# Two cross attentions on one core: another order of GpSimd in the first body, another cut of the last two

## The reference

```
stage 0: q = x Wq + bq; k = ctx Wk + bk; v = ctx Wv + bv
         w = softmax(q k^T / sqrt(512), over the query rows)
         n = layernorm(w v + x) * gamma + beta
stage 1: Q = n Wq + bq; K = ctx Wk + bk; V = ctx Wv + bv
         out = n + softmax(Q K^T / sqrt(512), over the keys) V Wo + bo
```

## Time and profile before

| | us |
|---|---|
| median of 3 runs | 681.7 |
| lowest, highest | 680.34, 682.13 |
| the profiled execution | 679.73 |
| its span | 677.8 |
| TensorE busy in the span | 666.5 |
| VectorE, GpSimd, ScalarE busy | 518.8, 490.5, 425.8 |

### The profile page before, as it was taken

How to read it: one execution, slowest core, us unless ns; L and a number is a source line. 1 busy time by engine, 2 the same in 40 slices (tenths; PEclk the granted TensorE clock), 3 DMA queues, 4 the chain that set the end, 5 groups by cost and what they waited for, 6 DMA issues and landing times.

```text
span 677.8 us, 12474 instructions
## 1 busy us (share of the span) xinstructions
PE 666.5 (98%) x4085; PEld 590.3 (87%) x4085; DVE 518.8 (77%) x1224; ACT 425.8 (63%) x1040; POOL 490.5 (72%) x394
## 2 busy tenths in 40 slices
PE   8998999999999999999999999999999999999997
PEld 7976988988898898889889898988989898888975
DVE  4978787877878687787968777796877779687764
ACT  4676657576665756666565666656566665666542
POOL 0387968779595877859687786958778695966771
PEclk9999999999999999999999999999999999999999
DMA  8902105050310405031040504004050401302003
GB/s 288 316 3 78 32 1 172 1 171 0 113 58 4 166 0 170 0 127 43 12 158 0 170 0 140 30 22 148 0 170 0 151 20 37 134 0 78 1 1 124
DMA packets 35585, 53.21 MB, mean 79 GB/s; under 512 B 5616, under 2 KB 13808, under 8 KB 35568
## 3 DMA queue, kind: packets, MB, share of 16 engines
q1 hardware_dynamic: 35568, 53.00, 23.7%
HBM read 36.18 MB, written 16.81 MB: 78 GB/s over the span
## 4 chain that ended last, share of the span: by engine, by line
PE 91%; POOL 4%; DVE 3%; issue 1%; DMA 1%; ACT 1%; SPq 0%; POOLq 0%; ACTq 0%; DVEq 0%
PE bank L424 79%; PE bank L431 12%; POOL n L1306 1%; POOL xprod L1333 1%; DMA wq_sb<-in_L_xattn_Wq_dram 1%; POOL wq_sb L1311 1%; POOL x_even L1347 0%; DVE rb L1059 0%; POOL cn_even_lo L1297 0%; POOL prod L1324 0%; DVE wv_sb L963 0%; DVE stats L1132 0%; POOL y_lo L1339 0%; POOL rstd L1317 0%; DVE x_even L1127 0%
## 5 line engine op out<-in xcount | busy, mean ns | idle before, releaser
L1324 POOL TENSOR_TENSOR prod<-n,u_b 128x512 f32<-128x512 f32 x64 | 81.5, 1295 | 40.1 <-DVE n L1143 39.2
L937 DVE SCALAR_TENSOR_TENSOR y_lo<-bank,terms,y_hi 128x512 fp32r<-128x512 f32 x64 | 47.9, 748 | 62.6 <-ACT y_hi L725 62.6
L1363 POOL TENSOR_TENSOR r<-r,beta_b 128x512 f32<-128x512 f32 x60 | 75.8, 1296 | 0.0
L1356 POOL TENSOR_TENSOR r<-n,gamma_b 128x512 f32<-128x512 f32 x60 | 75.5, 1286 | 0.1
L1317 POOL TENSOR_TENSOR rstd<-var_eps,minus_half 128x2 f32<-128x2 f32 x32 | 22.4, 699 | 65.4 <-DVE var_eps L1139 65.4
L725 ACT ACTIVATE y_hi<-bank,terms 128x512 fp32r<-128x512 f32 x64 | 43.9, 687 | 39.2 <-PE bank L424 39.2
L727 ACT ACTIVATE pc_hi<-bank 128x512 fp32r<-128x512 f32 x32 | 19.2, 600 | 68.4 <-PE bank L424 68.4
L813 ACT ACTIVATE bank<-e,neg 128x256 f32<-128x256 f32 x64 | 30.0, 469 | 37.9 <-DVE neg L1078 37.9
L424 PE MATMUL bank<-xT_hi,wqk_hi 128*128 128x512 f32 x128 | 51.2, 400 | 2.5 <-DVE xT_lo L939 2.5
L1116 DVE SCALAR_TENSOR_TENSOR r<-bank,rinv,r 128x512 f32<-128x512 f32 x60 | 44.8, 747 | 8.8 <-PE bank L424 8.8
L424 PE MATMUL bank<-wv_hi,wc_hi 128*128 128x512 f32 x128 | 51.5, 402 | 0.0
(11 more groups left out here) (214 smaller groups left out, 2381.4 us busy)
## 6 DMA issues: line engine op xcount, KB each, us to landing
out_dram<-r SPq DMA_DIRECT2D x15, 1024.0 KB, 5.5
x_even<-in_x_dram SPq DMA_DIRECT2D x8, 1024.0 KB, 7.3
ctxn<-in_ctx_dram SPq DMA_DIRECT2D x16, 512.0 KB, 3.7
x_odd<-in_x_dram SPq DMA_DIRECT2D x8, 1024.0 KB, 7.1
rb<-r_rows SPq DMA_DIRECT2D x15, 256.0 KB, 4.1
wq_sb<-in_L_xattn_Wq_dram SPq DMA_DIRECT2D x4, 256.0 KB, 5.2
wv_sb<-in_L_xattn_Wv_dram SPq DMA_DIRECT2D x2, 512.0 KB, 8.1
wq_sb<-in_L_xattn_Wq_dram SPq DMA_DIRECT2D x1, 1024.0 KB, 11.8
```

The lines of the kernel that those rows point to most:

```text
L937: i = dve.scalar_tensor_tensor(dst, src, bias, high.bitcast(F32), ALU.add, ALU.subtract)
L1324: pool.tensor_tensor(prod[j % 2][:], N[:, j, :], u_b[1][:], ALU.mult).then_inc(prod_ready, 1)
L1356: pool.tensor_tensor(r[:, j, :], N[:, j, :], gamma_b[:], ALU.mult).then_inc(scaled_ready, 1)
L1363: pool.tensor_tensor(r[:, j, :], r[:, j, :], beta_b[:], ALU.add).then_inc(resid_ready, 1)
```

## The change

On GpSimd the fourth column product of the first body goes to the other three; the larger sum of `bvwo` goes ahead of the first `rstd`, the smaller one behind it; the row products go ahead of the second `rstd`. VectorE's `finish_beta` of the first body goes to its end, and two preparation tiles take banks 6 and 7.

In the body before last `out` 0 is computed with its high products first, `n` of blocks 0 and 1 comes from ScalarE as rstd * x + shift, where VectorE makes shift = -mean * rstd. In the last body `late` 2 is computed in two halves, one ahead of and one behind the scores, the first quarter of the scores starts with its high products, `late` 3 takes bank 4, both low parts of `pt` go ahead of its output, and the last tile is computed, finished and stored in two halves of 256 columns in two banks.

```diff
--- before.py
+++ after.py
@@ -52,7 +52,7 @@
 PREP1B = tiles("wqk1", 2)
 PREP1C = [("wvo", 0), ("u1", 0), ("c1", 0), ("wvo", 1), ("bo1", 0)]
 
-PREP_BANKS = (7, 0, 1, 2, 3, 4, 5, 6) + (0, 1, 2, 3, 4, 5) + (2, 3, 6, 7) + (3, 1, 0, 5, 4)
+PREP_BANKS = (7, 0, 1, 2, 3, 4, 5, 6) + (0, 1, 2, 3, 4, 5) + (2, 3, 6, 7) + (3, 1, 0, 6, 7)
 
 
 def place_banks():
@@ -88,11 +88,12 @@
 FIRST = PREP0 + FIRST
 
 LATE = (1, 2, 3)
-BANK["late", 1], BANK["late", 2], BANK["late", 3] = 5, 0, 1
+BANK["late", 1], BANK["late", 2], BANK["late", 3] = 5, 0, 4
 BEFORE_LAST = [t for t in STEADY if t[0] != "out" or t[1] not in LATE]
 LAST = insert_after([t for t in STEADY if t[0] not in FRONT], ("nT", 3), [("late", 1)])
 LAST = insert_after(LAST, ("y1", 1), [("late", 2)])
-LAST = insert_after(LAST, ("pt", 0), [("late", 3)])
+LAST = insert_after(LAST, ("pt", 0), [("late", 3)]) + [("end", 0)]
+BANK["end", 0] = 0
 
 
 class Iteration:
@@ -241,7 +242,7 @@
         stats = sb("stats", [P, J, 6])
         mv = sb("mv", [P, J, 2])
         var_eps = sb("var_eps", [P, J])
-        rstd = sb("rstd", [P, J])
+        rstd, shift = sb("rstd", [P, J]), sb("shift", [P, RT])
         waited = sb("waited", [P, 2])
         minus_half = sb("minus_half", [P, J])
 
@@ -272,6 +273,7 @@
         bias_ready, x_biased = sem("bias_ready"), sem("x_biased")
         stats_ready, mv_ready = sem("stats_ready"), sem("mv_ready")
         var_ready, rstd_ready, n_ready = sem("var_ready"), sem("rstd_ready"), sem("n_ready")
+        shift_ready = sem("shift_ready")
         prod_ready, r1_ready = sem("prod_ready"), sem("r1_ready")
         negmx1_ready, neg1_ready, rinv1_ready = sem("negmx1_ready"), sem("neg1_ready"), sem("rinv1_ready")
         scaled_ready, resid_ready = sem("scaled_ready"), sem("resid_ready")
@@ -392,14 +394,19 @@
                     for j in range(J):
                         wait_emptied(sp, *((it, "late", j) if j in LATE else (before_last, "out", j)))
                     sp.dma_start(rows_of(out_rows, (PAIRS - 2) * J * P), R[:]).then_inc(rows_in_or_stored, 16)
-                    for j in range(J):
+                    for j in range(J - 1):
                         wait_emptied(sp, it, "out", j)
                         start = ((PAIRS - 1) * J + j) * P
                         sp.dma_start(out_rows[start:start + P, :], residual_of(it)[:, j, :]).then_inc(last_stored, 16)
+                    start = (PAIRS * J - 1) * P
+                    for tile, cols in ((("out", J - 1), slice(0, D // 2)), (("end", 0), slice(D // 2, D))):
+                        wait_emptied(sp, it, *tile)
+                        sp.dma_start(out_rows[start:start + P, cols], residual_of(it)[:, J - 1, cols])\
+                            .then_inc(last_stored, 16)
 
             run(sp, iteration)
             sp.wait_ge(rows_in_or_stored, 16 * (ROWS + PAIRS - 1))
-            sp.wait_ge(last_stored, 16 * J)
+            sp.wait_ge(last_stored, 16 * (J + 1))
 
 
         @block.tensor
@@ -602,12 +609,23 @@
             def scores1(it):
 
                 ct = CT[1 - it.parity]
-                for c in range(KC):
-                    wait_emptied(pe, it, "y1", c)
+                if it.last:
+                    pe.wait_ge(hi["y1"], it.times(KC, 0))
+                else:
+                    for c in range(KC):
+                        wait_emptied(pe, it, "y1", c)
                 for b in range(2):
                     dst = begin(it, "s1", b)
                     for tt in range(RT):
                         t0 = b * T + tt * P
+                        if it.last and (b, tt) == (0, 0):
+                            part = dst[:, 0:M]
+                            high, low = [h[:, :, t0:t0 + P] for h in Y1]
+                            product(part, [(high[:, c, :], h[:, c, 0:M]) for c in range(KC) for h in ct], last=False)
+                            for c in range(KC):
+                                wait_emptied(pe, it, "y1", c)
+                            product(part, [(low[:, c, :], ct[0][:, c, 0:M]) for c in range(KC)], first=False)
+                            continue
                         terms = []
                         for c in range(KC):
                             terms += passes([h[:, c, t0:t0 + P] for h in Y1],
@@ -654,6 +672,37 @@
                     terms += passes([h[:, b, ct, tt * P:(tt + 1) * P] for h in left], [h[:, ct, :] for h in right])
                 end(product(dst[:], terms), name, j)
 
+            def late_half(it, j, ct):
+
+                b, tt = divmod(j, RT)
+                dst = begin(it, "late", j) if ct == 0 else at(("late", j))
+                mm = product(dst[:], passes([h[:, b, ct, tt * P:(tt + 1) * P] for h in PC],
+                                            [h[:, ct, :] for h in WVO]), first=ct == 0, last=ct == KC - 1)
+                if ct == KC - 1:
+                    end(mm, "late", j)
+
+            def first_output(it):
+
+                pe.wait_ge(hi["pc"], it.times(2, 1 - 2))
+                dst = begin(it, "out", 0)
+                left = [[h[:, 0, ct, 0:P] for h in PC] for ct in range(KC)]
+                right = [[h[:, ct, :] for h in WVO] for ct in range(KC)]
+                product(dst[:], [(l[0], r[n]) for l, r in zip(left, right) for n in range(2)], last=False)
+                wait_emptied(pe, it, "pc", 0)
+                end(product(dst[:], [(l[1], r[0]) for l, r in zip(left, right)], first=False), "out", 0)
+
+            def last_output(it):
+
+                j = J - 1
+                b, tt = divmod(j, RT)
+                for tile, cols in ((("out", j), slice(0, D // 2)), (("end", 0), slice(D // 2, D))):
+                    dst = begin(it, *tile)
+                    terms = []
+                    for ct in range(KC):
+                        terms += passes([h[:, b, ct, tt * P:(tt + 1) * P] for h in PC],
+                                        [h[:, ct, cols] for h in WVO])
+                    end(product(dst[:, cols], terms), *tile)
+
             def iteration(it):
                 begin_it = it.j is None and it.known == 0
                 if begin_it:
@@ -679,13 +728,16 @@
                 if it.back:
                     project(it, "y1", "nT", WQK[1], NT)
                 if it.last:
-                    apply(it, "late", 2, "pc", PC, WVO)
+                    wait_emptied(pe, before_last, "pc", 1)
+                    late_half(it, 2, 0)
                 if it.front:
                     weigh0(it, 0)
                     row_sums(it)
                     weigh0(it, 1)
                 if it.back:
                     scores1(it)
+                if it.last:
+                    late_half(it, 2, 1)
                 if it.front:
                     if begin_it:
                         pe.wait_ge(wv0_ready, 1)
@@ -708,8 +760,13 @@
                 if begin_it:
                     prepare1c(it)
                 if it.back:
-                    for j in range(LATE[0] if it.before_last else J):
-                        apply(it, "out", j, "pc", PC, WVO)
+                    if it.before_last:
+                        first_output(it)
+                    else:
+                        for j in range(J - 1 if it.last else J):
+                            apply(it, "out", j, "pc", PC, WVO)
+                    if it.last:
+                        last_output(it)
 
             pe.wait_ge(consts_ready, 1)
             warm_up(0, 5)
@@ -837,6 +894,15 @@
                 wait_emptied(act, it, "rs")
                 act.activation(bias[j], bv0_b[:], ACT.Copy, scale=rs[:, j:j + 1]).then_inc(bias_ready, 1)
 
+            def normalise_first_rows(it):
+
+                wait_filled(act, it, "nT", KD - 1)
+                act.wait_ge(scaled_ready, it.times(J, 0))
+                act.wait_ge(shift_ready, 1)
+                for j in range(RT):
+                    act.activation(N[:, j, :], XN[it.parity][:, j, :], ACT.Identity, scale=rstd[:, j:j + 1],
+                                   bias=shift[:, j:j + 1]).then_inc(n_ready, 1)
+
             def row_terms(it, blocks, back):
 
                 for j in blocks:
@@ -916,6 +982,8 @@
                         round_bank(it, "pt", b, halves(PT[0], b))
                     for b in range(2):
                         round_bank(it, "pc", b, halves(PC[0], b))
+                        if it.before_last and b == 0:
+                            normalise_first_rows(it)
                 if it.more and it.back:
                     next_row_terms0(it)
                 if it.front and it.back and not it.before_last:
@@ -1116,6 +1184,15 @@
                 dve.scalar_tensor_tensor(r[:, j, :], at((name, j))[:], rinv1[:, j:j + 1], r[:, j, :],
                                          ALU.mult, ALU.add).then_inc(emptied[BANK[name, j]], 1)
 
+            def last_output(it):
+
+                r = residual_of(it)
+                for tile, cols in ((("out", J - 1), slice(0, D // 2)), (("end", 0), slice(D // 2, D))):
+                    wait_filled(dve, it, *tile)
```

(31 more changed lines are left out.)

## The result

| | before | changed |
|---|---|---|
| median of 20 runs | 681.49 us | 686.89 us |
| lowest, highest | 680.06, 682.13 | 680.17, 690.75 |
| profiled execution, span | 679.73, 677.8 | 689.38, 687.4 |

The ratio is 1.0051, 95% interval 1.0033 to 1.0069: slower. It leaves out the changed kernel's three runs over 690.5 us, which by their clock are more of what follows (the medians of all runs stand at 1.0079), as the ratios further down leave out two runs of before at 892 and 952 us with mean clocks of 0.70 and 0.66.

A forecast was written before the change was run, and what follows sets the result against it. TensorE was taken as the bound, busy 666.5 of 677.8 us, so only its 11.3 us of standing counted. First body -0.1 and last bodies +0.1 gave 0.0, so 681.7, stated as 681.8 for restarts; range 679.2 to 684.1.

The forecast's parts named there:

- The meeting on GpSimd's port: First body: VectorE's second dot product waits out GpSimd's 128x1024 sum, ends at 52.94; TensorE stalls 2.98 us before spreading `u1`.
- The first body without a fall: First body at full clock: 2.5 us stall goes, 3.0 us stall comes, `y` at 63.4 instead of 63.44; sum -0.1 us.
- The body before last: `out` 0 high products first, two normalisations on ScalarE: all behind comes 0.65 us earlier, bounds -1.2 and 0.
- The held output: Last body: VectorE's `output(2, late)` holds the first maximum; transposes of `e` at 663.98 after a 3.0 us stall; step costs 1.38.
- The last tile: End of last body: two half outputs and stores; last matmul at 675.32, end at 677.87 against 677.8, +0.1 us.
- The sum without a fall: Whole kernel at full clock: first body -0.1 us plus last bodies +0.1 us gives 0.0 us, 681.7 again.
- Rival C: TensorE's clock falls behind the 3.0 us stalls: 683.3 once, 684.8 in both; chance 0.2 once, 0.1 twice.
- The base: Whole run: sum made in the profiled execution (679.73 us), its 1.97 us difference to the 681.7 median added.

The follow-up runs named there:

- the waits filled: Changed kernel with 11 and 12 added 128x512 matmuls in TensorE's waits for `terms` and `e`: median 680.30 us, ratio 0.9988.
- the sum behind `rstd`: Changed kernel with GpSimd's 128x1024 sum of `bvwo` put back behind the first `rstd`: median 680.36 us, ratio 0.9988.
- output behind maxima: Changed kernel with VectorE's output of `late` 2 moved behind `maxima1` in the last body: median 678.69 us, ratio 0.9982.
- last bodies alone: Kernel before with only the changes of the last two bodies, first body as before: median 682.16 us, ratio 1.0023.
- Dense work behind the wait: Changed kernel with 16 added 128x512 matmuls directly behind the wait for `terms`, ahead of the spread of `u1`: median 684.86 us, ratio 1.0050.
- before, wait filled: Kernel before with 9 added 128x512 matmuls ahead of the transposes of `x_odd`, in the wait for `xT_lo`: median 679.85 us, ratio 0.9980.
- both moved: Changed kernel with the 128x1024 sum behind the first `rstd` and VectorE's output of `late` 2 behind `maxima1`: median 676.58 us, ratio 0.9938.
- sum waits, output moved: Changed kernel with the 128x1024 sum waiting for `terms` and VectorE's output of `late` 2 behind `maxima1`: median 676.51 us, ratio 0.9936.

## Why the prediction was wrong

Foretold were 681.8 us, in a range of 679.2 to 684.1; measured are 686.89. Step by step:

- **The meeting on GpSimd's port: right.** Foretold: 0.14 us apart, dot product to 52.94, a wait of 2.98. Measured: 0.17, 52.74, 2.66.
- **The first body without a fall: right.** `y` at 63.4 foretold, 63.51 with the waits filled. The normalisations took 1.94 us.
- **The body before last: nearly.** ScalarE's two normalisations took 1.51 us, 0.2 more than assumed; the transposes' wait for `n` was 0.6, as counted. The transposes were to start 0.65 us earlier; with the waits filled they start at 647.62 instead of 648.07, so 0.45 earlier.
- **The held output: right.** Transposes of `e` at 663.98 foretold, 664.24 with the waits filled; a wait of 3.0, measured 2.81. Taken out, some 3 us came back: without a fall 676.5 to 677.5 against 679.3 to 680.2, the sum behind `rstd` in both.
- **The last tile: right.** From the transposes of `e` to the end 13.9 us foretold, 14.0 with the waits filled.
- **The sum without a fall: right.** 0.0 against before; measured 680.2 to 680.4 in three runs, and 680.30 with the waits filled, against 679.3 to 680.4 (median 680.11) in the 17 runs of before at full clock.
- **Rival C: the right mechanism, mis-sized, and this is the step that failed.** The sum had nothing for the clock, and the rival had: "if the low level stays over 3 us of work behind a stall, 1.5 us are lost". In the first body of the profiled run it stayed for 17.1 us and 7.9 us were lost, over the rival's own bound of 5 too. I took the length of the stall for that of the fall; nothing in the trace of before spoke to it. For the short kind the 1.5 was right: over the same work with and without one, the traces show 1.4 us (last body, changed), 1.5 (first body, output behind maxima) and 1.6 (`y`, last bodies alone). The chance was too low as well: "it held over 2.5 us without work" came from one execution, where 17 of the changed kernel's 20 runs have a clock of 0.997 or less, and three quarters of the runs of before too.
- **The base.** I added 1.97 us between the profiled execution and the median as a constant. Some 1.3 us of it was a fall in the median's runs, so the forecast added a stall to a kernel that already paid for one. Two runs that differ by more than their usual scatter were a clue that was in the times: 680.34 against 681.70 and 682.13.

Open: why a fall of the same kernel is short in some runs and long in others. Dense work behind the wait speaks for itself in six runs, no more; which of the sparse work behind the wait (one-column products, float32 products, transposes) keeps it low was not separated. What made the clock fall at 8.9 us, behind waits of under 0.9 us, is open too.

## What to carry to other kernels

In this kernel a wait of TensorE has two prices: its own length, and the clock behind it. A reordering that swaps one wait of 2.5 us for another is neutral in the first and can lose 8 us in the second, when sparse work follows; look at what stands behind the wait, and fill it with dense matmuls if it can't be removed. When a matmul group is moved behind another, move its reader in the other engine's order too. And before costing an instruction of VectorE that reads SBUF at its usual time, look at what GpSimd then runs; two SBUF inputs aren't needed, as `normalise` and `var_eps` show. Last, tell two waits for the same tile apart by their lines before comparing them.

## What the runs showed of the hardware

- The clock fell to 1.2 GHz around waits of 2.5 to 2.8 us, not in every run, and in one trace at 8.9 us behind waits of 0.8 and 0.9 us. The four kernels whose longest wait is 1.1 us or less (both waits filled; before, wait filled; both moved; sum waits, output moved) have 0.999 or 1.000 in all 33 runs.
- The short falls ahead of the last matmul last 3.4 us wherever a trace has one and cost 1.4 to 1.6 us there; the medians of the runs at 0.997 or 0.998 lie 0.8 to 1.7 us above those at full clock. The two long ones in traces lasted 17.1 us over sparse work. With 16 matmuls of 128x512 behind the wait none of six runs had a long one.
- A fall can begin after the wait is over: 0.9 us (53.92 against 53.00) in the changed kernel, 1.5 us (54.95 against 53.49) with the dense work behind it.
- Beside a GpSimd sum a 128x4 operation with two SBUF inputs took 1.09 us instead of 0.16, and a 128x2 one with a single SBUF input 1.52 instead of 0.17: small instructions waited for the end of the sum as well.
